# A two-layer transformer step on one core: the first gate group's normalisation on VectorE, and two residual steps placed behind the third group's statistics

## The reference

```
h = layernorm(x) * (1 + ca) + sa                    # per token; ca, sa from the conditioning
Q, K, V = h @ Wq + bq, h @ Wk + bk, h @ Wv + bv     # 16 heads of 8
attn = softmax(causal(Q K^T / sqrt(8)))
d = h @ dp_w1 + dp_b1                               # 64 wide
d = (d - mean) / sqrt(var + 1e-5) * ln_g + ln_b     # <- the step that changes engine for some tokens
drift = gelu(d) @ dp_w2 + dp_b2                     # one number per token
gate = tanh(gelu(drift * g_w1 + g_b1) @ g_w2 + g_b2)
out = (attn * gate) @ V @ Wo + bo                   # the gate scales a key's value row
x = x + ga * out
```

## Time and profile before

| what | value |
|---|---|
| median of three timed runs | 961.76 us |
| the profiled execution's own time | 962.33 us |
| its span (first to last instruction) | 960.6 us |
| mean granted PE clock | 0.978 |
| busy PE / DVE / ACT / POOL | 900.8 / 700.0 / 634.9 / 367.0 us |
| PE busy share, 300 to 900 us | 0.97 to 1.00 |

### The profile page before, as it was taken

How to read it: one execution, slowest core, us unless ns; L and a number is a source line. 1 busy time by engine, 2 the same in 40 slices (tenths; PEclk the granted TensorE clock), 3 DMA queues, 4 the chain that set the end, 5 groups by cost and what they waited for, 6 DMA issues and landing times.

```text
span 960.6 us, 17779 instructions
## 1 busy us (share of the span) xinstructions
PE 900.8 (94%) x6420; PEld 638.7 (66%) x6420; DVE 700.0 (73%) x1889; ACT 634.9 (66%) x1103; POOL 367.0 (38%) x439
## 2 busy tenths in 40 slices
PE   4598998989999999999999999999999999999996
PEld 3354554545567888777777777776777566999982
DVE  7986787886579968686877878687885865643664
ACT  6477778776687766667767777777777566654420
POOL 4365145140001101242545517255361515268881
PEclk9687999999999999999999999999999999999999
DMA  5845343654042125210211111110111513022327
GB/s 132 236 127 137 95 125 104 184 152 128 16 133 63 37 54 139 68 42 26 67 44 45 45 45 45 44 66 23 56 55 27 173 45 110 26 71 81 87 71 241
DMA packets 86179, 83.15 MB, mean 87 GB/s; under 512 B 8978, under 2 KB 72456, under 8 KB 86092
## 3 DMA queue, kind: packets, MB, share of 16 engines
q1 hardware_dynamic: 80868, 73.33, 26.9%
q0 software_dynamic: 4320, 8.27, 2.6%
q10 hardware_dynamic: 904, 0.42, 0.1%
HBM read 50.54 MB, written 31.72 MB: 86 GB/s over the span
## 4 chain that ended last, share of the span: by engine, by line
PE 68%; DVE 21%; ACT 5%; issue 3%; DMA 2%; SPq 1%; POOL 0%; POOLq 0%; DVEq 0%; ACTq 0%
PE psum L1582 18%; PE psum L1624 10%; PE psum L1605 6%; PE psum L1619 6%; PE psum L1420 4%; DVE pieces L2121 3%; PE psum L1359 3%; DVE maxes L1998 3%; PE psum L1402 2%; PE psum L1539 1%; PE psum L1375 1%; PE psum L1329 1%; PE psum L1496 1%; DVE tmp L2186 1%; DVE gb_tok L2136 1%
## 5 line engine op out<-in xcount | busy, mean ns | idle before, releaser
L1582 PE MATMUL psum<-parts,q_stack 128*128 128x512 f32 x640 | 250.3, 472 | 1.7 <-DVE parts L2318 1.0
L2620 ACT ACTIVATE big<-psum,cols 128x512 f32<-128x512 f32 x205 | 140.1, 688 | 75.3 <-PE psum L1582 72.9
L2848 POOL TENSOR_TENSOR hT<-hT,gb_tok 128x512 f32<-128x512 f32 x54 | 75.9, 1405 | 265.2 <-DVE gb_tok L2136 264.2
L1582 PEld LDWEIGHTS psum<-parts,q_stack 128*128 128x128 f32 x640 | 111.7, 190 | 52.9 <-issue 39.5
L1998 DVE TENSOR_REDUCE maxes<-psum 128x4 f32<-128x1024 f32 (+1 forms) x96 | 114.5, 1216 | 28.9 <-PE psum L1375 28.4
L1582 PE MATMUL psum<-parts,k_stack 128*128 128x512 f32 x320 | 126.1, 394 | 0.0
L1624 PE MATMUL psum<-big,ew 128*128 128x512 f32 x232 | 118.4, 593 | 0.0
L1619 PE MATMUL psum<-pieces,w_parts 128*128 128x512 f32 x336 | 97.8, 399 | 0.0
L2928 POOL DMA_INDIRECT routed<-big,slot_i x64 | 65.5, 1023 | 52.6 <-DVE slot_i L2305 31.1
L2121 DVE TENSOR_TENSOR pieces<-big,pieces 128x512 fp32r<-128x512 f32 x89 | 76.2, 862 | 10.9 <-ACT pieces L2627 10.9
L2951 POOL DMA_INDIRECT answers<-hT,to x64 | 62.6, 979 | 34.5 <-DVE hT L2333 19.2
(11 more groups left out here) (432 smaller groups left out, 1889.7 us busy)
## 6 DMA issues: line engine op xcount, KB each, us to landing
gb_tok<-gate_rows SPq DMA_DIRECT2D x32, 512.0 KB, 3.7
q_stack<-q_pieces SPq DMA_DIRECT2D x32, 192.0 KB, 3.4
k_stack<-k_pieces SPq DMA_DIRECT2D x32, 192.0 KB, 4.4
routed<-empty_row SPq DMA_DIRECT2D x4, 1040.0 KB, 10.0
big<-routed SPq DMA_DIRECT2D x16, 260.0 KB, 3.1
answers<-empty_row SPq DMA_DIRECT2D x4, 1024.0 KB, 6.2
q_pieces<-gb_tok SPq DMA_DIRECT2D x16, 192.0 KB, 2.1
k_pieces<-gb_tok SPq DMA_DIRECT2D x15, 192.0 KB, 2.1
```

The source lines that it names most:

```text
L1582: last = eng.matmul(bank(i), w1_part(wp, e)[:, fs], parts[2 * xk + xp][:, :], start=n == 0, stop=n == 2)
L2620: eng.activation(slots[held("slot", "up", n, e, f)], bank(held("bank", "up", n, e, f)), ACT.Relu, bias=col("L0_ffn_b1", e * FC + f)).then_ ...
L2848: eng.tensor_tensor(hT[:, ns], xpT[:, ns] if e == 0 else hT[:, ns], gate_wide[:, e // GHELD % 2, e % GHELD, :], ALU.add).then_inc(sem("acc ...
```

## The change

`gv_a` of gate group 0 goes away. Its three instructions become a new step `gv_n 0` on DVE. The groups 1 to 3 keep `gv_a` on POOL. `rest 1 0` and `rest 1 1`, the first subtractions of chunk 1, get `stat 0 0 2` as one more thing they come after. Two costs in the planner are lowered: `gv_s 0` from 3.2 to 2.4 and `stat 0 0 2` from 2.2 to 1.8. The text of the waits follows through the helper `scaled(n)`.

```
+SCALED_BY_DVE = 1
+def scaled(n):
+    return ("gv_n", n) if n < SCALED_BY_DVE else ("gv_a", n)
...
-        p.step("stat", 0, 0, g, work="dve:2.2", urgent=4 if g == 1 else 20 if g == 0 else BACK, after=[("moment", b) for b in range(t0 // TPB, t1 // TPB)])
+        p.step("stat", 0, 0, g, work="dve:1.8" if g == 2 else "dve:2.2", urgent=4 if g == 1 else 20 if g == 0 else BACK, after=[("moment", b) for b in range(t0 // TPB, t1 // TPB)])
...
-                p.step("rest", n, w, work="pool:1.2", urgent=3, after=[("proj", n, w)], tmp=tile)
+                p.step("rest", n, w, work="pool:1.2", urgent=3, after=[("proj", n, w)] + ([("stat", 0, 0, 2)] if n == 1 else []), tmp=tile)
...
-        p.step("gv_s", n, work="dve:3.2", urgent=0 if n else 8, after=[("gv_q", n)], tmp=tile)
-        p.step("gv_a", n, work="pool:3.7", urgent=4 if n else 8, after=[("gv_s", n), ("rows",)], tmp=tile)
-        p.step("gv_g", n, work="act:3.2", urgent=4 if n else 8, after=[("gv_a", n)], tmp=tile)
+        p.step("gv_s", n, work="dve:3.2" if n else "dve:2.4", urgent=0 if n else 8, after=[("gv_q", n)], tmp=tile)
+        p.step(*scaled(n), work="dve:1.9" if n < SCALED_BY_DVE else "pool:3.7", urgent=4 if n else 8, after=[("gv_s", n), ("rows",)], tmp=tile)
+        p.step("gv_g", n, work="act:3.2", urgent=4 if n else 8, after=[scaled(n)], tmp=tile)
...
+            def gv_n(n):
+                t3 = T(held("tmp", "gv_n", n))[:, :].rearrange("p (t n) -> p t n", n=HID)
+                ts = slice(n * GT, (n + 1) * GT)
+                w.wait_ge(*done("gv_s", n))
+                eng.tensor_tensor(t3, vd[:, ts, C:VW], drs[:, ts].unsqueeze(2).to_broadcast([P, GT, HID]),
+                                  ALU.mult).then_inc(chain.sem, chain.more())
+                w.wait_ge(rows_in, ROWS_LATER)
+                w.wait_ge(chain.sem, chain.n)
+                eng.tensor_tensor(t3, t3, row("L0_attn_ln_g").unsqueeze(1).to_broadcast([P, GT, HID]),
+                                  ALU.mult).then_inc(chain.sem, chain.more())
+                w.wait_ge(chain.sem, chain.n)
+                eng.tensor_tensor(t3, t3, row("L0_attn_ln_b").unsqueeze(1).to_broadcast([P, GT, HID]),
+                                  ALU.add).then_inc(sem("gv_n"), 1)
```

More of the change, by code:

```diff
@@ L175 @@
     "val": ("value", "pe dve"), "proj": ("project", "pe act dve"), "rest": ("cut", "pool"), "cut": ("cut", "act pool"), "write": ("write", ""),
-    "center": ("setup", "dve"), "gv_q": ("gate", "act"), "gv_s": ("gate", "dve"), "gv_a": ("gate", "pool"), "gv_g": ("gate", "act"),
+    "center": ("setup", "dve"), "gv_q": ("gate", "act"), "gv_s": ("gate", "dve"), "gv_a": ("gate", "pool"), "gv_n": ("gate", "dve"), "gv_g": ("gate", "act"),
     "gv_w": ("gate", "pool"), "gv_d": ("gate", "dve"), "gv_h": ("gate", "act"), "gv_r": ("gate", "dve"),
@@ L524, in order_steps @@
     early_over = [pieces_done(NCH - 1, 1), pieces_done(NCH - 1, 0), ("gv_r", NT // GT - 1), *[("ln_t", 0, 0, b) for b in range(B)]]
-    values_over = [gated, *[("gv_a", n) for n in range(NT // GT)]]
+    values_over = [gated, *[scaled(n) for n in range(NT // GT)]]
     p.step("values_over", after=values_over,
@@ L1212, in wraw @@
                 for n in range(NT // GT):
-                    w.wait_ge(*done("gv_a", n))
+                    w.wait_ge(*done(*scaled(n)))
                 eng.dma_start(w_raw[:, 0:3, :], a["L1_attn_qkv_w"].rearrange("(g p) c -> p g c", p=P)).then_inc(raw_in, 16)
@@ L2382, in sum_ @@
                 eng.tensor_tensor(x[:, ts, :], x[:, ts, :], both, ALU.add).then_inc(sem("sum"), 1)
-            mine = {"head_rows": head_rows, "head_cols": head_cols, "mod": mod, "moment": moment, "stat": stat, "ln_z": ln_z, "val": val, "proj": proj, "center": center, "gv_s": gv_s,
+            mine = {"head_rows": head_rows, "head_cols": head_cols, "mod": mod, "moment": moment, "stat": stat, "ln_z": ln_z, "val": val, "proj": proj, "center": center, "gv_s": gv_s, "gv_n": gv_n,
                     "gv_d": gv_d, "gv_r": gv_r, "max": max_, "mrow": mrow, "turn": turn, "bo": bo,
```

## The result

The changed kernel took 971.38, 972.09, 972.98 and 976.27 us, median 972.54; the kernel before, in the same runs, 961.09. The ratio is 1.0121, 95% interval 1.0103 to 1.0138: slower by 11.4 us. The forecast was 958.6, range 952 to 967. So the local part came out as forecast, and the time went the other way. The profiled execution after took 971.38, its span is 969.2, its mean granted clock 0.973.

The account below looks back on a forecast made before the run. PE was taken to bound the kernel, short of work mostly before 96 us. Terms -2.2 - 1.0 + 0 = -3.2 us took the profiled 962.33 to 959.1, as a median 958.6; range 952 to 967.

Parts of the forecast that it names:

- Part 1: gv_s 0 and stat 0 0 2 on DVE, free of POOL: 4.20 us instead of 10.72, giving back 6.5.
- Part 2: gv_n 0 on DVE beside rest 1 0 and rest 1 1: 4.30 us for all five instructions by turns.
- Part 3: First maxima on DVE start between 36.05 and 36.35 instead of 38.57; 2.2 us earlier taken, at worst 0.8 later.
- Part 4: On PE up to 54 us: all 2.2 us carried on; chunk 1's writes, 2.4 us later, costed at nothing.
- Part 5: PE's hole before 86.11 us and half clock to 94: gain of 1 us, bounds -7 to +2.3.
- Part 6: Later attention, gate group 3 earlier and all four fills ahead of mrow 11: 0 us, between -3 and +9.
- rival B: Weight fills on SP's queue make mrow 11's reader wait: net 11.3 - g, 967.9 at g = 2; chance 0.15.
- g: Time in us between the first weight fill and mrow 11 on SP's queue, estimated near 8.
- a little for disorder in the many moved steps: Unsized allowance for the many moved steps; with rival B it made up the 0.16 chance of slower.
- Rival C: rest 1 x meets gv_n 0 and the writes' 2.4 us reach mrow 0; gain spent, 961.8; chance 0.15.

Follow-up runs that it names:

- e7: e1 with a true semaphore wait on GpSimd: rest 1 0 and rest 1 1 run only when stat 0 0 2 is done; ratio 1.0000.
- e1: Kernel before, its order kept, without the dependency and cost edits; gv_n 0 put on VectorE, gv_w 0 behind rest 1 1; 959.26 us, ratio 0.9973.
- e11: e1 again, unchanged, in a later session; 979.72 us, ratio 0.9963 to the kernel before.
- e4: Changed kernel with fills 2 and 3 moved on SP's queue from ahead of mrow 11 to behind stack 15; 966.16 us, ratio 1.0059.
- e6: Changed kernel with a true wait on GpSimd: rest 4 0 and rest 4 1 run only when stat 0 0 4 is done; ratio 1.0115.
- e5: Changed kernel with gate group 3's first step held for batch 10's first scores, which also moves fills 2 and 3 later; ratio 1.0049.
- e12: e10 with fills 0 and 1 moved on SP's queue from ahead of mrow 12 to behind it; ratio 0.9994.
- e13: e10 with all four weight fills moved on SP's queue behind mrow 14; 975.11 us, ratio 0.9896.
- e10: e7 with both cut steps of chunk 1 ahead of gv_w 0 on GpSimd; 976.45 us, ratio 0.9945.
- e8: Changed kernel with the edits of e5 and e6 together; 988.33 us, ratio 1.0041.

## Why the prediction was wrong, step by step

- Part 1, the collision: the premise failed, the effect was near. "With `rest 1 x` held until the statistics are done": nothing holds it. Two collisions stayed, and the statistics ended at 34.0, not 32.05: 4.5 us given back instead of 6.5. This cost nothing, since `gv_n 0` then ran alone.
- Part 2, the cost of `gv_n 0`: 2.1 us in the changed kernel, without the company that the part expected. Beside `rest`, in e7, `gv_n 0` was done 3.86 us after it began at 32.23, `rest` 3.31 after; the sum by turns had said 4.30 for all five. The bounds held. The trace agrees here with the rule of the Trainium skill that was cited ("SBUF — State Buffer", "Who interferes with whom"): the two VectorE instructions that met `rest` took 1.51 and 1.53 us instead of 0.69.
- Part 3, the first maxima: the number was right, 36.16 for 36.05 to 36.35, but by luck. The part had DVE free at 34.1 to 36.35 and PE's scores as the floor at 36.05. The scores ended at 34.97 + 0.66 = 35.63, because the stacks landed 0.42 us earlier, and what the maxima waited for was `gv_n 0`, which began 2 us later than forecast and took its shortest time.
- Part 4, "Whether the 2.2 us reach PE": failed. I followed the bank chain on PE and VectorE and the row on SP, and did not put ScalarE's list beside them, where a second half of `proj 2` had moved ahead of the first exponential; it had on PE's list too. 0.40 of 2.41 us came through. With the lists of before, on ScalarE and elsewhere (e1), the first exponential came 3.37 us earlier in the profiled execution, 2.54 in e11.
- Part 5, the second hole: 1 us was forecast, and no gain is to be seen. The hole is at 84.6 to 88.8 us now, in five short waits; 86 to 94 us has 6.46 us busy at 0.58 for 7.89 at 0.50.
- Part 6, the rest of the attention, is the step that failed and decided. "I take 0" stood for +13 (972.54 less e1's 959.26; 14 by the ratios). Its bound of +9 came from rival B, which had the right place (the reader of batch 11's row) and the wrong mechanism: B summed bandwidth, 15.7 us of transfers less 5 less g, and the estimate of g near 8 made the sum small. That estimate was good: from the first fill at 198.78 to the row ready at 205.84 are 7.1 us, by which B gives a wait of 3.6. It was 7.34. What was late was the sending: ready at 205.84, sent at 211.79. From sending to its reader it then took 5.4 us, less than batch 12's row took before (210.78 to 217.08). The issue of one fill had held the queue with the row behind it. That is 6 us of the time (e4). About 7 us more (e4 less e1) lie in the new order. They show before `mrow 11`, which PE reaches at 207.44 us in e4 and at 192.30 in e1, in the profiled executions: between 96 and 200 us PE is busy 92.93 us at 0.94 of the clock in e4, and 97.96 at 1.00 in e1. This is what I had called "a little for disorder in the many moved steps". Of its two visible places, the wait that removes the collision at `stat 0 0 4` won nothing (e6), and keeping the gate groups apart won nothing that can be told beyond the fills (e5). The sum is shown, its parts are not.
- Rival C, "the collision only moves", was right in kind: not to `gv_n 0`, but to a statistics step 90 us later.

The test that I had named, PE's idle time between 96 and 200 us growing by more than 3, came out at 6.5.

## What to carry to other kernels

Where a planner writes the order, time an edit first with the old lists held fixed: here the edit was worth -2 us and the lists that it brought +13. A dependency in the planner is not a wait in the program; read the function before counting on it. And put the large transfers of a queue where the gap to the next small one on it is longer than their issue at its worst, not at its shortest.

## What the runs showed of the hardware

The issue of a 1 MB fill on SP took from 0.72 to 8.48 us for the same instruction. The table has the fourth fills. Its last column is when the last transfer sent on SP ahead of the third fill had landed, that is, when its data had arrived:

| run | third fill starts | fourth starts | its issue | it ends | all ahead of the third landed |
|---|---|---|---|---|---|
| e6 | 206.15 | 207.43 | 8.48 | 215.91 | 216.09 |
| changed kernel | 202.21 | 203.50 | 8.25 | 211.75 | 211.92 |
| e12 | 210.80 | 213.58 | 6.38 | 219.97 | 220.15 |
| e13 | 235.26 | 236.54 | 5.99 | 242.53 | 242.46 |
| e4 | 222.78 | 224.07 | 3.92 | 227.99 | 226.67 |
| e10 | 209.72 | 216.44 | 1.52 | 217.95 | 218.17 |
| e8 | 221.22 | 224.07 | 1.35 | 225.41 | 225.75 |
| e5 | 223.14 | 226.71 | 1.13 | 227.84 | 227.11 |
| e1 | 208.60 | 215.34 | 0.72 | 216.06 | 216.01 |
| kernel before | 214.24 | 221.97 | 0.72 | 222.69 | 221.80 |

The time since the third fill does not settle it alone: e12 and e8 have 2.8 us between the two and issues of 6.38 and 1.35. The landings do better. Where the transfers ahead of the third fill had landed by the end of a short issue, the fourth took 0.72 us (0.72 to 0.76 in the six runs that the table leaves out), about what the third does (0.83). Where they had not, it was held, and in six of the eight held ones it ended within 0.4 us of the last of those landings, in e5 and e4 by 0.7 and 1.3 us later. So an issue is held while much of what was sent before is under way; that the queue has a limit on it is the reading that fits, and no run here measured that limit.
